# Attention two groups ahead, Newton runs for two groups, reordered routing steps, short POOL pauses, and expert products three blocks ahead

## The chip, the cores and the metric

The kernel runs on one core of one Trainium2 chip. The metric is the time on the device in microseconds (us). TensorE is called PE here, VectorE DVE, ScalarE ACT, GpSimd POOL and SyncE SP, as in the profile.

## The reference, cut to what matters

Activations are 64 x 64 tokens of width 128 (4096 tokens), all in float32.

```
K = ctx;  Q = layernorm(x)
scores = tril(K K^T)                        # per batch entry of 64 tokens, no softmax
x = x + tanh(g_xattn) * (Q + scores Q)
z = layernorm(x)
shared = silu(z sw1^T) sw2^T                # hidden width 512
top 2 of z gate_w^T over 8 experts; gates = softmax of the two logits
expert_e = silu(z w1_e^T) w2_e^T            # hidden width 512
x = x + tanh(g_ffn) * (shared + sum over the two experts of gate * expert_e)
```

Only the two chosen experts count for a token, so the kernel sends token rows to per-expert regions, multiplies whole blocks of 128 rows of one expert, and sends the rows back.

## The kernel before, in words

The 4096 tokens are 32 tiles of 128, in 8 groups of 4 tiles. There is a **first stage** (attention, layernorm, routing and the shared expert) and an **expert stage** of 71 blocks of 128 rows.

*First stage, PE* (`score`, `apply_scores`, `transpose_n`, `logits`, `positions`, `shared_units`). Each of 8 steps s runs apply_scores(s+1), transpose_n(s), score(s+2), logits(s), positions(s) and seven "units". A unit is one quarter of a group's shared expert: an even one is an up product (`ps_sup`), an odd one a down product (`ps_so`) of the group before. There are 72 units in all; `units_of(step)` deals them out, 7 a step from step 1. What is left runs after step 7, and units 64 to 71 (four down products) run between the first up products of the expert stage. `keep_warm` matmuls fill holes at the start.

*First stage, DVE* (one queue, in program order, step s): `residual(s+1)` (attention output added, statistics of the sum), `mask_scores(s+2)`, `choose(s)` (copy the logits out of PSUM, top 8, indices, one-hot, a running count), `statistics1(s+3)`, `norms` (a Newton run for 1/sqrt, 13 small instructions each waiting for the last, for the first layernorm of group s+3 and the second one of group s+1), and `place(s)`, which turns PE's `positions` into row numbers (`slot`) and releases POOL. The first groups' 1/sqrt runs on POOL (`norm`).

*First stage, ACT*: `centre_and_scale(g)` writes q, `normalise(g)` writes n, `evacuate_nT`, and `after_units` (silu of the up products, copies of the shared result into `shared`).

*POOL* scatters rows of n to DRAM, one indirect DMA for each tile and expert choice (`scatter_x`), with a `pause` (a memset of `spacer`, 128x400, on whose end the queue waits) after every second one. Groups 0 to 3 have 8 scatters each, groups 4 to 7 have 4 (together 48, part 0); 12 more of part 1 follow and four are spread over the expert stage. There `scatter_y(b)` sends the result rows of a block back.

*Between the stages.* After `place(7)` DVE runs `count_rows`, `place_second`, `tables_full` (rows and experts of the first 40 blocks; `tables_done` 1) and `tables_rest` (the others). SP waits for `tables_done`, loads the weights w1 of four blocks, waits until all 48 part-0 scatters have landed (`x_scattered[0]`), loads the rows of blocks 0 to 3 (`load_x(0)`), two more w1, then `load_x(1)` and `load_x(2)`. A set is four blocks; `transpose_rows(s)` transposes its rows and `evacuate_xT(s)` (DVE) copies them out of PSUM.

*Expert stage, PE*: transposes of set 0, up(0), up(1), units 64 to 71, transposes of set 1, a wait for all of `shared_out`, and then for each block b up(b+2) and down(b). `silu` and `evacuate_y` are ACT's. The last output groups are loaded, added and stored at the end.

Names and lines that matter: L426 pause, L420 scatter_x, L293 load_w1, L302 load_x, L615 residual, L607 mask_scores, L630 the logits copy, L572 statistics, L592 to L599 norms, L664 the first instruction of place, L674 and L676 the slots, L709 the end of a table, L776 evacuate_xT, L818 score, L828 apply_scores, L835 transpose_n, L844 logits, L869 and L877 units, L919 transpose_rows, L935 up, L944 down.

## Time and profile before

| | |
|---|---|
| three runs, us | 281.13, 277.95, 277.69; median 277.95 |
| the profiled execution, us | 278.51, of it 276.8 between first and last instruction (the span) |
| PE / PE weight loads busy | 244.2 us (88%) / 215.4 us (78%) |
| DVE / ACT / POOL busy | 129.4 (47%) / 132.0 (48%) / 178.4 us (64%) |
| mean granted PE clock | 0.949 |
| chain that ended last, by engine | PE 73%, DVE 10%, issue 5%, ACT 3%, POOL 3%, DMA 2%, unknown queue 2% |
| DMA | 46.94 MB, mean 170 GB/s |

The chain is the work followed back from the last instruction. The busy shares are means over two stages that differ, so they are to be read by stretch. A granted clock of 1.00 is 2.4 GHz, 0.50 is 1.2 GHz.

### The profile page before, as it was taken

How to read it: one execution, taken by the hardware profiler on the slowest of the kernel's cores; microseconds unless marked ns; L12 is line 12 of the kernel's file. 1: busy time of each engine (PE TensorE's matmuls, PEld its weight loads, DVE VectorE, ACT ScalarE, POOL GpSimd, SP SyncE). 2: the span in 40 equal slices, each digit the busy share in tenths (PEclk: the TensorE clock that was granted, in tenths of full speed). 3: DMA queues.
4: the chain of work that ended last, by engine and by line, in shares of the span. 5: the costliest groups of instructions: out<-in, count | busy, mean ns of one | idle time of the engine just before them, and what ended most of it. 6: DMA issues, size and time to landing. Idle time of an engine off the chain costs nothing.

```text
span 276.8 us, 6393 instructions
## 1 busy us (share of the span) xinstructions
PE 244.2 (88%) x1805; PEld 215.4 (78%) x1805; DVE 129.4 (47%) x576; ACT 132.0 (48%) x293; POOL 178.4 (64%) x249
## 2 busy tenths in 40 slices
PE   8789478999799799984999999999999999999910
PEld 4566266778578477784999999999999999999810
DVE  3959968678867668711321122223221101148203
ACT  1573262554545444422455456555555565555510
POOL 5674878668754367874678888887776545455430
PEclk9979979689889999998999999999999999999995
DMA  6992111111110011865766777776777767899827
GB/s 209 402 375 90 39 51 45 45 41 39 40 41 20 20 43 48 242 166 136 199 150 203 227 229 227 214 228 208 211 217 218 227 206 199 243 279 370 303 67 266
DMA packets 32625, 46.94 MB, mean 170 GB/s; under 512 B 5472, under 2 KB 16480, under 8 KB 32336
## 3 DMA queue, kind: packets, MB, share of 16 engines
q1 hardware_dynamic: 27264, 35.45, 42.7%
q0 software_dynamic: 4320, 8.99, 9.2%
q10 hardware_dynamic: 1008, 2.10, 2.0%
q8 instruction: 16, 0.26, 0.4%
q14 instruction: 17, 0.14, 0.2%
HBM read 34.43 MB, written 12.09 MB: 168 GB/s over the span
## 4 chain that ended last, share of the span: by engine, by line
PE 73%; DVE 10%; issue 5%; ACT 3%; POOL 3%; DMA 2%; another core or an unknown queue 2%; SPq 0%; POOLq 0%; DVEq 0%
PE bank L935 23%; PE bank L944 23%; PE bank L877 7%; PE bank L869 7%; PE bank L818 3%; PE bank L844 3%; PE bank L919 3%; ACT n L492 2%; PE bank L835 2%; DMA nT<-y_rows 2%; PE bank L884 1%; POOL rstd L378 1%; PE bank L828 1%; DVE top_at L636 1%
## 5 line engine op out<-in xcount | busy, mean ns | idle before, releaser
L452 POOL DMA_INDIRECT y_rows<-y,dest x71 | 69.9, 984 | 45.3 <-ACT y L548 30.6
L420 POOL DMA_INDIRECT expert_rows<-n,slot x64 | 63.1, 985 | 35.2 <-issue 15.9
L935 PE MATMUL bank<-xT,w_ring 128*128 128x128 f32 x568 | 76.2, 278 | 5.5 <-ACT kT L509 3.6
L944 PE MATMUL bank<-w,hT 128*128 x568 | 75.6, 277 | 0.0
L935 PEld LDWEIGHTS bank<-xT,w_ring 128*128 128x128 f32 x568 | 69.8, 194 | 6.5 <-issue 6.4
L944 PEld LDWEIGHTS bank<-w,hT 128*128 128x128 f32 x568 | 69.8, 194 | 0.0
L542 ACT ACTIVATE hT<-bank 128x512 f32<-128x512 f32 x71 | 42.4, 597 | 39.8 <-PE bank L935 27.0
L776 DVE COPY xT<-bank 128x512 f32<-128x512 f32 (+1 forms) x18 | 12.3, 684 | 98.4 <-PE bank L919 53.5
L877 PEld LDWEIGHTS bank<-sw,sT 128*128 128x128 f32 x256 | 33.5, 196 | 11.1 <-issue 11.1
L548 ACT ACTIVATE y<-bank,gate 128x128 f32<-128x128 f32 x71 | 26.1, 367 | 23.0 <-PE bank L944 13.6
L877 PE MATMUL bank<-sw,sT 128*128 128x128 f32 x256 | 34.5, 281 | 0.0
L869 PE MATMUL bank<-nT,sw 128*128 128x512 f32 x64 | 34.4, 625 | 0.0
L506 ACT ACTIVATE sT<-bank 128x512 f32<-128x512 f32 x32 | 19.0, 593 | 30.0 <-PE bank L869 26.1
L426 POOL MEMSET spacer<- 128x400 f32 x70 | 31.2, 446 | 0.1
L492 ACT ACTIVATE n<-xres,shift,rstd 128x128 f32<-128x128 f32 x32 | 13.2, 482 | 15.8 <-DVE shift L599 8.6
L835 PE MATMUL bank<-ident,n 128*128 128x128 f32 x32 | 9.2, 335 | 9.2 <-issue 5.3
L572 DVE BATCH_NORM_STATS2 stats<-xres 128x6 f32<-128x128 f32 x64 | 13.9, 280 | 3.0 <-DMA xres<-in_xP 2.6
L835 PEld LDWEIGHTS bank<-ident,n 128*128 128x128 f32 x32 | 4.4, 146 | 13.3 <-issue 8.7
L482 ACT ACTIVATE q<-xres,shift,rstd 128x128 f32<-128x128 f32 x32 | 13.1, 482 | 2.7 <-POOL shift L379 2.7
L818 PEld LDWEIGHTS bank<-kT 128*128 128x128 f32 x64 | 12.3, 269 | 0.7
L792 DVE TENSOR_TENSOR xres<-xres,nT 128x512 f32<-128x512 f32 x8 | 5.5, 692 | 14.4 <-DMA nT<-y_rows 12.7
L818 PE MATMUL bank<-kT 128*128 128x128 f32 x64 | 12.1, 354 | 0.0
(124 smaller groups left out, 229.7 us busy)
## 6 DMA issues: line engine op xcount, KB each, us to landing
w_ring<-in_w1T SPq DMA_DIRECT2D x71, 256.0 KB
x_ring<-expert_rows SPq DMA_DIRECT2D x71, 66.0 KB
w<-in_w2T SPq DMA_DIRECT2D x2, 1024.0 KB, 15.7
kT<-y_rows SPq DMA_DIRECT2D x8, 256.0 KB
nT<-y_rows SPq DMA_DIRECT2D x8, 256.0 KB, 3.8
out<-xres SPq DMA_DIRECT2D x8, 256.0 KB
xres<-in_xP SPq DMA_DIRECT2D x3, 512.0 KB, 10.2
kT<-in_ctxT ACTq DMA_DIRECT2D x3, 512.0 KB, 10.8
```

What stands on the lines that cost most here:

```text
L420: pool.indirect_dma_start(out=x_dram[:, :], out_offset=bass.IndirectOffsetOnAxis(ap=slot[:, i, k:k + 1], axis=0), in_=n[:, i, :], in_offse ...
L426: chained(pool.memset(spacer[:, :], 0.0))
L452: pool.indirect_dma_start(out=y_dram[:, :], out_offset=bass.IndirectOffsetOnAxis(ap=dest[:, b:b + 1], axis=0), in_=y[:, j], in_offset=None ...
L506: act.activation(sT[:, g % 2, j // 2], ps_sup[i % 2][:, :], ACT.Silu).then_inc(sT_done, 1)
L542: act.activation(hT[:, b % UP_SLOTS], ps_up[b % UP_SLOTS][:, :], ACT.Silu).then_inc(hT_done, 1)
L548: act.activation(y[:, b % Y_RING], ps_y[b % 2][:, 0:D], ACT.Copy, scale=gate[:, b:b + 1]).then_inc(y_done, 1)
L818: last = pe.matmul(ps_s[:, t * P:(t + 1) * P], k_t, k_t, start=False, stop=(t == G - 1), skip_group_check=True)
L835: last = pe.transpose(ps_n[:, t * P:(t + 1) * P], n[:, g * G + t, 0:D], ident[:, :])
L869: pe.matmul(ps_sup[i % 2][:, :], sw1[:, j // 2 * P:(j // 2 + 1) * P], nT[:, group(g)], start=True, stop=True).then_inc(sup_psum, 1)
L877: last = pe.matmul(ps_so[(g - 1) % 2][:, cols], sT[:, (g - 1) % 2, c, cols], sw2[:, c * D:(c + 1) * D], start=(c == 0), stop=(c == HC - 1))
L935: last = pe.matmul(ps_up[b % UP_SLOTS][:, cols], w1_ring[:, b % W_RING, cols], xT[:, s % X_SETS, i * P:(i + 1) * P], start=True, stop=True)
L944: last = pe.matmul(ps_y[b % 2][:, 0:D], hT[:, b % UP_SLOTS, c * P:(c + 1) * P], w2[:, ds(at + c * D, D)], start=(c == 0), stop=(c == HC - 1))
```

## The change

* Inputs: the loads of context groups 2 to 7 move from ACT's queue to SP's, and SP issues everything from group 2 on only when x of group 1 has landed.
* DVE: `choose` reads the logits from PSUM without the copy. Attention runs two groups ahead (`residual(s+2)`, `mask_scores(s+3)`). `norms` works on two groups at a time, in odd steps only. In even steps the order is choose, mask, residual, place, statistics of two groups; in odd steps residual, norms, choose, mask, place. `tables_rest` moves behind `evacuate_xT(0)`.
* PE: apply_scores(s+2) and score(s+3) in step s. Units begin in step 0: `UNTIL` puts 7, 14, 20, 27, 33, 40, 46, 52 of them behind the steps 0 to 7 (before: 0, 7, 14, 21, 28, 35, 42, 49). In odd steps all seven stand ahead of `positions`, in even ones three. 28 warm matmuls (8, 8, 3, 5, 4) in place of 29 (8, 5, 6, 10).
* POOL: a pause after every scatter, of 128x100. SP: two w1 loads ahead of `load_x(0)` instead of four and six behind it (the ring has 8 slots); the fills of region ends come one in two blocks from block 4.
* Expert stage: up products three blocks ahead, three PSUM banks for down products (`Y_SLOTS`), one bank instead of two for row transposes, transposes six blocks ahead; the wait for the last `shared_out` moves to block 1.

The diff, cut ("..." marks what is left out):

```diff
-    W_RING = 6
+    W_RING = 8
...
-    UP_AHEAD = 2
+    UP_AHEAD = 3
+    Y_SLOTS = 3
...
-    T_AHEAD = 5
+    T_AHEAD = 6
...
-    PER_STEP = 7
+    UNTIL = (7, 14, 20, 27, 33, 40, 46, 52)
...
-            return range((step - 1) * PER_STEP, min(UNITS * (GROUPS + 1), step * PER_STEP)) if step < GROUPS \
-                else range((GROUPS - 1) * PER_STEP, UNITS * (GROUPS + 1))
+            return range(UNTIL[step - 1] if step else 0, UNTIL[step])
...
+                if i == 2:
+                    sp.wait_ge(x_in[1], 16)
...
+                if i >= 2:
+                    sp.dma_start(kT[:, a * GW:b * GW], ctxT[:, a * GW:b * GW]).then_inc(ctx_in[i], 16)
...
-            for b in range(SET):
+            for b in range(2):
...
-            for b in range(SET, W_RING):
+            for b in range(2, W_RING):
...
-            sp.wait_ge(end_row_done, 1)
-            sp.wait_ge(tables_done, 2)
...
             for b in range(USED):
...
-                if b < E:
-                    fill_end(b)
+                if b == 4:
+                    sp.wait_ge(end_row_done, 1)
+                if b % 2 == 0 and 0 <= b // 2 - 2 < E:
+                    fill_end(b // 2 - 2)
...
+                        sp.wait_ge(tables_done, PARTS)
...
+            norm2(1)
...
-            norm2(1)
...
-                    if i % 2 == 1:
-                        pause()
+                    pause()
...
-                if i % 2 == 1:
-                    pause()
+                pause()
             def scatter_y(b):
...
+            act.dma_start(kT[:, GW:2 * GW], ctxT[:, GW:2 * GW]).then_inc(ctx_in[1], 16)
...
-            for i in range(1, len(LOADS)):
-                a, b = LOADS[i][0] * GW, LOADS[i][1] * GW
-                act.dma_start(kT[:, a:b], ctxT[:, a:b]).then_inc(ctx_in[i], 16)
...
+            centre_and_scale(2)
             for s in range(GROUPS):
...
-                if in_range(s + 2):
-                    centre_and_scale(s + 2)
-                some = units_of(s) if s > 0 else range(0)
-                after_units(some[:PER_STEP - 2])
-                if in_range(s + 1):
-                    normalise(s + 1)
-                after_units(some[PER_STEP - 2:])
-            after_units(range((GROUPS - 1) * PER_STEP, UNITS * GROUPS))
+                some = units_of(s)
+                if s % 2 == 0:
+                    if s == 0:
+                        normalise(1)
+                    if in_range(s + 3):
+                        centre_and_scale(s + 3)
+                    after_units(some[:4])
+                    if s > 0 and in_range(s + 1):
+                        normalise(s + 1)
+                else:
+                    after_units(some[:4])
+                    if in_range(s + 1):
+                        normalise(s + 1)
+                    if in_range(s + 3):
+                        centre_and_scale(s + 3)
+                after_units(some[4:])
+            after_units(range(UNTIL[-1], UNITS * GROUPS))
...
-                act.activation(y[:, b % Y_RING], ps_y[b % 2][:, 0:D], ACT.Copy, scale=gate[:, b:b + 1]).then_inc(y_done, 1)
-            for b in range(UP_AHEAD):
+                act.activation(y[:, b % Y_RING], ps_y[b % Y_SLOTS][:, 0:D], ACT.Copy, scale=gate[:, b:b + 1]).then_inc(y_done, 1)
+            for b in range(UP_AHEAD - 1):
...
+            silu(UP_AHEAD - 1)
             for b in range(USED):
...
-            def norms(slot, kinds):
-                out, var = rstd[:, slot, kinds], var_eps[:, slot, kinds]
-                bits, sq = half_bits[:, kinds], square[:, kinds]
-                chained(dve.tensor_scalar(var, mv[:, slot, kinds, :, 1], EPS, None, ALU.add))
+            def norms(slots, kinds):
+                out, var = rstd[:, slots, kinds], var_eps[:, slots, kinds]
+                bits, sq = half_bits[:, :, kinds], square[:, :, kinds]
+                chained(dve.tensor_scalar(var, mv[:, slots, kinds, :, 1], EPS, None, ALU.add))
...
-                return dve.scalar_tensor_tensor(out=shift[:, slot, kinds], in0=mv[:, slot, kinds, :, 0], scalar=-1.0,
+                return dve.scalar_tensor_tensor(out=shift[:, slots, kinds], in0=mv[:, slots, kinds, :, 0], scalar=-1.0,
...
-                dve.tensor_copy(logit[:, j], ps_logit.rearrange("p (t e) -> p t e", e=E)).then_inc(logit_read, 1)
-                dve.wait_ge(logit_read, g + 1)
...
-                    dve.max(out=top[:, g * G + t, :], in_=logit[:, j, t, :]).then_inc(top_done, 1)
+                    dve.max(out=top[:, g * G + t, :], in_=ps_logit[:, t * E:(t + 1) * E]).then_inc(top_done, 1)
...
-                    dve.max_index(out=top_at[:, j, t, :], in_max=top[:, g * G + t, :], in_values=logit[:, j, t, :])\
+                    dve.max_index(out=top_at[:, j, t, :], in_max=top[:, g * G + t, :], in_values=ps_logit[:, t * E:(t + 1) * E])\
...
-            mask_scores(0)
...
+            mask_scores(0)
+            mask_scores(1)
+            residual(0)
+            for_power(second(0)).then_inc(stats2_done, 1)
...
-            residual(0)
-            for_power(second(0)).then_inc(stats2_done, 1)
-            mask_scores(1)
+            residual(1)
+            for_power(second(1)).then_inc(stats2_done, 1)
+            mask_scores(2)
...
             for s in range(GROUPS):
-                if in_range(s + 1):
-                    residual(s + 1)
-                if s == 0:
-                    for_power(second(1)).then_inc(stats2_done, 1)
-                if in_range(s + 2):
-                    mask_scores(s + 2)
-                choose(s)
-                if s > 0 and in_range(s + 3):
-                    statistics1(s + 3)
-                    norms(s + 3, slice(0, 2)).then_inc(newton, 1)
-                elif s > 0 and in_range(s + 1):
-                    norms(s + 3, slice(0, 1)).then_inc(newton, 1)
-                place(s)
+                if s % 2 == 0:
+                    choose(s)
+                    if in_range(s + 3):
+                        mask_scores(s + 3)
+                    if in_range(s + 2):
+                        residual(s + 2)
+                    place(s)
+                    for g in (s + 4, s + 5):
+                        if in_range(g):
+                            statistics1(g)
+                else:
+                    if in_range(s + 2):
+                        residual(s + 2)
+                    if in_range(s + 1):
+                        norms(slice(s + 3, s + 5), slice(0, 2) if in_range(s + 3) else slice(0, 1)).then_inc(pairs_done, 1)
+                    choose(s)
+                    if in_range(s + 3):
+                        mask_scores(s + 3)
+                    place(s)
...
-            tables_rest()
             def evacuate_xT(s):
...
-                dve.tensor_copy(xT[:, s % X_SETS, 0:blocks * P], ps_x[s % 2][:, 0:blocks * P]).then_inc(xT_done, 1)
+                dve.tensor_copy(xT[:, s % X_SETS, 0:blocks * P], ps_x[:, 0:blocks * P]).then_inc(xT_done, 1)
...
+                    if b + T_AHEAD == 0:
+                        tables_rest()
...
+            keep_warm(8)
+            score(1)
+            apply_scores(0)
+            keep_warm(3)
+            apply_scores(1)
+            score(2)
...
-            apply_scores(0)
-            score(1)
-            keep_warm(6)
             for s in range(GROUPS):
-                if in_range(s + 1):
-                    apply_scores(s + 1)
+                some = units_of(s)
+                if s % 2 == 1 and in_range(s + 2):
+                    apply_scores(s + 2)
...
-                if in_range(s + 2):
-                    score(s + 2)
-                some = units_of(s) if s > 0 else range(0)
-                early = 0 if in_range(s + 2) else 1
-                shared_units(some[:early])
+                if s == 0:
+                    keep_warm(4)
+                elif in_range(s + 3):
+                    score(s + 3)
+                else:
+                    shared_units(some[:1])
...
-                    keep_warm(10)
-                shared_units(some[early:4])
+                    score(3)
+                rest = some if in_range(s + 3) else some[1:]
+                if s % 2 == 0 and in_range(s + 2):
+                    apply_scores(s + 2)
+                early = 7 if s % 2 == 1 and in_range(s + 2) else 3
+                shared_units(rest[:early])
...
-                shared_units(some[4:6])
...
+                    shared_units(rest[early:early + 2])
...
-                shared_units(some[6:])
-            shared_units(range((GROUPS - 1) * PER_STEP, UNITS * GROUPS))
+                    shared_units(rest[early + 2:])
+                else:
+                    shared_units(rest[early:])
+            shared_units(range(UNTIL[-1], UNITS * GROUPS))
             def transpose_rows(s):
-                at_least(pe, xT_done, s - 1)
+                at_least(pe, xT_done, s)
...
-                    last = pe.transpose(ps_x[s % 2][:, i * P:(i + 1) * P], x_ring[:, j, 0:D], ident[:, :])
+                    last = pe.transpose(ps_x[:, i * P:(i + 1) * P], x_ring[:, j, 0:D], ident[:, :])
...
-                at_least(pe, y_done, b - 1)
+                at_least(pe, y_done, b - Y_SLOTS + 1)
...
-                    last = pe.matmul(ps_y[b % 2][:, 0:D], hT[:, b % UP_SLOTS, c * P:(c + 1) * P], w2[:, ds(at + c * D, D)],
+                    last = pe.matmul(ps_y[b % Y_SLOTS][:, 0:D], hT[:, b % UP_SLOTS, c * P:(c + 1) * P], w2[:, ds(at + c * D, D)],
...
-            for b in range(UP_AHEAD):
+            for b in range(UP_AHEAD - 1):
...
-            pe.wait_ge(shared_out, GROUPS)
+            pe.wait_ge(shared_out, GROUPS - 1)
+            up(UP_AHEAD - 1)
             for b in range(USED):
...
+                if b == 1:
+                    pe.wait_ge(shared_out, GROUPS)
...
```

## Rows read from the trace of the kernel before

**Rows 1.** Windows (stretch, length, busy us of each engine, granted clock, DMA share, GB/s).
```profile
117.00:133.00 16.00, 11.66 (x88) 11.22 (x87) 2.52 (x10) 4.34 (x9) 9.86 (x13) 0.89 0.64 159
133.00:262.00 129.00, 127.84 (x1141) 127.30 (x1141) 35.25 (x100) 72.44 (x169) 87.97 (x112) 1.00 0.76 231
```

**Rows 2.** Timeline of PE (start, us, line, operation, count; idle before): step 4, full clock.
```profile
61.50 1.05 PE L828 MATMUL bank<-q,scores 128*128 128x128 f32 x8
62.39 0.60 PE L835 MATMUL bank<-ident,n 128*128 128x128 f32 x4
62.83 0.38 PE L814 MATMUL bank<-ident 128*128 128x512 bf16 x1
...
63.94 0.96 PE L844 MATMUL bank<-gT,nT 128*128 128x8 f32 x8
64.75 1.14 PE L877 MATMUL bank<-sw,sT 128*128 128x128 f32 x8
65.72 1.02 PE L869 MATMUL bank<-nT,sw 128*128 128x512 f32 x2
```

**Rows 3.** Timeline of DVE: step 2, from one residual to the next.
```profile
35.87 0.74 DVE L615 SCALAR_TENSOR_TENSOR xres<-bank,tanh_g,xres 128x512 f32<-128x512 f32 x1
...
39.77 0.69 DVE L607 TENSOR_TENSOR scores<-bank,mask 128x512 f32<-128x512 f32 x1 [1.84 <-PE bank L818]
40.76 0.19 DVE L630 COPY logit<-bank 128x32 f32<-128x32 f32 x1 [0.30 <-PE bank L844]
...
45.35 0.17 DVE L592 TENSOR_SCALAR var_eps<-mv 128x8 f32<-128x8 f32 x1
...
47.97 0.18 DVE L664 TENSOR_TENSOR where<-bank,region_row 128x32 f32<-128x32 f32 x1
...
48.63 0.74 DVE L615 SCALAR_TENSOR_TENSOR xres<-bank,tanh_g,xres 128x512 f32<-128x512 f32 x1
```

**Rows 4.** Timeline of PE, then the window around it (columns as in rows 1).
```profile
48.73 1.39 PE L835 MATMUL bank<-ident,n 128*128 128x128 f32 x4 [1.61 <-ACT n L492]
...
48.00:54.00 6.00, 5.16 (x22) 4.34 (x23) 3.77 (x19) 4.20 (x10) 3.88 (x6) 0.70 0.12 38
```

**Rows 5.** Timeline of POOL: a small memset, the first scatter, and two scatters with their pause.
```profile
3.12 0.20 POOL L369 MEMSET mask<- 128x128 f32 x1
...
24.34 1.19 POOL L420 DMA_INDIRECT expert_rows<-n,slot  x1 [2.77 <-DVE slot L674]
...
50.76 0.96 POOL L420 DMA_INDIRECT expert_rows<-n,slot  x1 [0.31 <-issue]
51.72 0.45 POOL L426 MEMSET spacer<- 128x400 f32 x1
...
53.71 0.96 POOL L420 DMA_INDIRECT expert_rows<-n,slot  x1 [0.30 <-issue]
```

**Rows 6.** Timelines of DVE, SP and PE between the two stages.
```profile
102.58 0.19 DVE L676 TENSOR_REDUCE slot<-placed 128x4 int32<-128x32 f32 x1
...
116.33 0.17 DVE L709 TENSOR_SCALAR weight_at<-expert_of 1x31 int32<-1x31 f32 x1
...
109.39 2.87 SPq L293 DMA_DIRECT2D w_ring<-in_w1T  x4
112.99 2.53 SPq L302 DMA_DIRECT2D x_ring<-expert_rows  x4
...
117.65 7.27 SPq L302 DMA_DIRECT2D x_ring<-expert_rows  x8
...
118.47 2.05 PE L935 MATMUL bank<-xT,w_ring 128*128 128x128 f32 x16 [0.78 <-issue]
...
128.09 1.34 PE L935 MATMUL bank<-xT,w_ring 128*128 128x128 f32 x8 [3.55 <-ACT kT L509]
```

**Rows 7.** The chain of waits near the end (start, us, what): a scatter's landing.
```profile
265.31 2.24 DMA y_rows<-y,dest
```

**Rows 8.** Timeline of POOL beside the table work: the longer of the two slow scatters.
```profile
112.40 1.65 POOL L420 DMA_INDIRECT expert_rows<-n,slot  x1 [0.28 <-issue]
```

18 lines of the change are left out of this document (8 added, 10 removed).

## The prediction

> **What bounds the kernel now.** I read the windows first. From 133 to 262 us PE is busy 127.84 of 129 us at a granted clock of 1.00: the expert stage is as dense as its matmuls allow, and nothing in the change takes a matmul out of it. In front of it, from 117 to 133 us, PE is busy 11.66 of 16 us [rows 1]. So time can come only from when the expert stage starts, and from the 14.8 us after it, which the change leaves alone.
>
> Then the timeline of PE in a step of the first stage. At full clock, start to start: apply_scores 0.89 (62.39 - 61.50), transpose_n 0.44, score 1.11, logits 0.81, together 3.25 us; a down unit 0.97 and an up unit about as much less a tenth, 0.9 us for a unit on the mean [rows 2]. With seven units a step needs 3.25 + 6.3 = 9.6 us of PE.
>
> The timeline of DVE for step 2 goes from 35.87 to 48.63, 12.76 us, of which it is idle 1.84 and 0.30: 10.6 us of work [rows 3]. So neither engine is full: DVE waits for PE's score and logits, and PE then waits for the normalised rows that hang on DVE's norms. A wait of PE of 1.61 us stands in front of a stretch with a granted clock of 0.70, so between two levels, 1.2 and 2.4 GHz, it lost 0.30 x 6 = 1.8 us more there [rows 4]. The steps from the first scatter (24.34) to the last slots (102.77) take (102.77 - 24.34)/7 = 11.2 us each [rows 5, 6]. That is what the change works on: the loss is a chain that runs from PE to DVE to ACT and back once a step.
>
> **The change part by part.**
>
> *DVE in a step.* The norms take 47.97 - 45.35 = 2.62 us; one run for two groups halves that, -1.31 us a step (16 elements instead of 8 in instructions of 0.17 us, which I take as free; bound: +0.05 us in each of 13). The logits copy goes, 40.76 to its end 0.19 and a gap, -0.2 us; max and index then read PSUM, bounded by nothing and by the 0.2 us saved. 10.6 - 1.5 = 9.1 us a step while attention runs, less in steps 4 to 7, where statistics and then residuals run out [rows 3].
>
> *PE in a step.* 3.25 + 0.9 x 6.5 = 9.1 us in the mean. So both engines need about 9.1 us, and running attention two groups ahead gives each something to do while the other is late. I walked the queues with these durations. Start: the input order and warm matmuls differ, but the chain statistics, POOL's 1/sqrt, q, attention, residual, n of group 0 keeps its length; the first slots come at 25.4, or 27 if the clock is half there; I take 26 against 24.0. Steps 1 to 3: DVE is full (9.1) and PE's score(s+3) waits once a pair of steps for mask_scores, 1.1 us, and positions waits 0.5 to 2 us for choose in odd steps: 10.3 us a step, last slots of group 3 at 57. Steps 4 to 7: PE bounds, 8.65 (six units), 2.14 + 6.3 = 8.4 (no score), and twice 1.25 + 5.4 = 6.65, less 1.8 us that PE is ahead by: 28.5 us. Slots of group 7 at 85.6, against 102.8.
>
> *POOL now bounds.* Two scatters and a pause take 53.71 - 50.76 = 2.95 us. A memset of 128x400 takes 0.45, one of 128x128 0.20, and one of 128x100 will be near 0.18 (bounds 0.10 and 0.20). A scatter with its pause: 0.96 + 0.18 + 0.28 (the gap behind a pause, 2.95 - 0.96 - 0.45 - 0.96 - 0.30) = 1.42 us, hardly less than the 1.48 of now. 48 of them from 26.3 on: 26.3 + 68.2 = 94.5, while the slots come early enough after group 1 to keep the queue fed [rows 5]. The last one lands 2.24 us later as a scatter does at the end of the kernel [rows 7]: 96.8. The other path to the first row loads: slots 85.6, tables 109.39 - 102.77 = 6.6, two w1 loads of 2.87/4 = 0.72: 93.7. So load_x(0) is issued at 96.8 (112.99 before) [rows 6]. Both paths are equal when slots of group 7 come at 88.3; later than that, every us counts.
>
> Two scatters of the trace are longer, 1.65 us at most, and both lie beside the table work of DVE [rows 8]; beside DVE's small instructions they take 0.96, and so the sum has 0.96 for all 48. The Trainium skill, SBUF — State Buffer, section "Who interferes with whom", says that a GpSimd instruction and a copy, cast or tensor_scalar of DVE in a two-port form shut each other out for the whole instruction. By it a fuller DVE would stretch POOL's chain, which now sets the end of the stage; by the rows nothing is added. What it would come to is rival C.
>
> *Between the stages.* PE's units after logits(7): 5 + 12 = 17, so 15 us, against 21 before; logits(7) ends near 81 and PE is through at 96: it idles until the rows land. Issue of four x loads 2.53 -> 99.3. Before, the last of them was issued by 115.5, and up(0) started at 118.47 after transposes (0.44) and the 0.78 of the copy, so a landing costs at most 118.47 - 1.22 - 115.5 = 1.7 us -> 101.0; transposes and copy 1.2 -> 102.2 [rows 6]. up(0) and up(1) take 2.05 less a tail, 1.8 us, at full clock and 3.6 at half; PE has idled 5 us before, so I take 3.0 -> 105.2. Units 64 to 71, four down products of 0.9: 108.8. Meanwhile SP issues six w1 (6 x 0.72 = 4.3) and set 1 (4 x 7.27/8 = 3.6) -> 107.2, landed 108.9, transposed 109.3. up(2) starts at 109.5, against 128.09 before: -18.6 us. tables_rest now lies behind the copy of set 0; it takes the time from the first table, which lets SP go at 109.39 or some tenths before, to 116.5, 7 to 8 us [rows 6], so from 102.2 to 110.2, and the copy of set 1 is done at 111.0; up(4), the first to need it, comes after up(2), up(3) and down(0) at 112.2: hidden with 1.2 us to spare, and if PE is earlier than that it costs the difference.
>
> *The clock behind it.* Before, the expert stage began at half clock after 3.55 us of idle; the stretch 117 to 133 shows 0.89, 1.8 us lost [rows 1, 6]. With up(2) right behind the units this is not paid: -1.8.
>
> *The unexplained wait.* PE's 3.55 us were charged to a copy by ACT that itself had nothing visible to wait for. By the arithmetic above set 1 was in by 117.65 + 3.6 + 1.7 = 123.0. I can't name it. Its bounds after the change are 0 and about 2.7 us; as the wait for the last shared_out moves behind two up products, I take 0.7.
>
> *Expert stage.* Three ahead, three banks, eight w1 slots: PE has 1.2 us of idle in 129 us, so at most that is gained; a block needs its x and w1 as many blocks ahead as before or more. One bank for the transposes asks DVE for a copy of 0.7 us every four blocks (7.6 us): nothing. The part-1 scatters follow at 94.5 and take 12 x 1.42 = 17 us, until 111.5; the first y is due at 112. Nothing.
>
> **The sum.** 276.8 - 18.6 - 1.8 + 0.7 = 257.1 span. The profiled execution takes 1.7 us more than its span (278.51) and stands 0.6 us above the median. 258.8 us. About 2%, 5.6 us, is what a measurement of this kernel can tell from no change.
>
> **The rivals.**
>
> *A, the clock.* The waits of PE in odd steps (up to 2 us) are of the size of the one that stood before the stretch at 0.70 [rows 4]. If six steps lose 1.8 us each, slots of group 7 come at 96.4, 8.1 behind the 88.3 from which it counts: 258.8 + 8.1 = 267. For it: it happens now. Against it: a wait of 1.1 us has no such row, and POOL covers the first 2.7 us. 19%.
>
> *B, the steps stay as long.* PE and DVE wait for each other in a ring, so that only the place of the waits moves. At 11.2 us a step slots of group 7 come at 26 + 78.4 = 104.4, load_x(0) at 112.5, up(2) at 125.2: 276.8 - 2.9 - 1.8 + 1.7 + 0.7 = 274.5. If DVE's 9.1 and PE's front part 3.25 lie wholly in line, 12.35 a step, it is 282.6. Both within 2% (the first by 0.6%). 10%, since the norms and the copy do leave DVE's queue.
>
> *C, slower: POOL's scatters stretch.* DVE would be nearly full, and two of 64 scatters, beside table instructions of 0.9 us, took up to 1.65 instead of 0.96 us [rows 8]. At +0.69 for each of 48 POOL ends at 94.5 + 33.1 = 127.6, and up(2) starts 33.1 later, at 142.6: 258.8 + 33.1 = 291.9. It is slower by 2% from +0.53 us each (25.3 us), that is if three scatters in four are hit. Against it: the other 62 scatters took 0.96 beside the same small instructions. 4%.
>
> *D, as forecast.* 67%, with a range of its own from 253 to 263: low with a pause of 0.10 us (-3.8, of which 3.1 until the tables bind), full clock at up(0) (-1.2) and some of the idle in the expert stage (-1); high with first slots at 27, the whole unexplained wait (+2) and a landing 1 to 2 us longer.
>
> **How the numbers follow.** The time is D's. The range 253 to 269 takes in D but for a twentieth and nearly all of A: about 8 in 10. Faster by over 2% are D and A, 0.86; within 2% is B, 0.10; slower is C, 0.04.
>
> **What the profile after would show.** POOL: scatters at a distance of 1.42 us without a gap from group 2 on, the 48th near 94 us; if slots of group 7 come after 88 and the scatters have gaps, A or B holds. DVE: one run of norms per two groups, instructions still 0.17 us; the span from residual to residual near 10 us in steps 1 to 3. load_x(0) at 97, up(2) at 109.5, the stretch behind it at a clock of 1.00, and 147.6 us from up(2) to the end (148.7 before). The prediction is wrong if load_x(0) waits for something else than the scatters' landing, if PE waits at set 1 for its w1 or rows, or if the expert stage shows idle that it did not have.

## The result, and the profile after

The changed kernel takes 281.12 us (median of 20 runs, 277.78 to 284.94) against 277.79 for the kernel before (20 runs, 274.82 to 281.13): ratio 1.012, 95% interval 1.009 to 1.015. It is slower by 1.2%, less than the 2% that the prediction took as what one measurement can tell, but twenty runs of each set it apart from no change; 258.8 us, faster by 7%, was forecast. Ratios, here and below, leave out executions more than 1.5% above the fastest of the same kernel. The profiled execution took 280.87 us, its span is 279.1.

The page of the changed kernel, part 1 (busy time, share and instructions of each engine):

```profile
PE 242.8 (87%) x1804; PEld 213.6 (77%) x1804; DVE 118.4 (42%) x529; ACT 129.3 (46%) x293; POOL 164.8 (59%) x279
```

DVE's work shrank from 129.4 to 118.4 us, as costed. The span did not. The hole opens in step 3 of the first stage. PE, DVE and ACT in the timelines of the changed kernel (start, duration, idle time before and what ended it):

```profile
46.11 1.06 PE L846 MATMUL bank<-q,scores 128*128 128x128 f32 x8
47.01 0.60 PE L853 MATMUL bank<-ident,n 128*128 128x128 f32 x4
...
47.66 1.05 PE L836 MATMUL bank<-kT 128*128 128x128 f32 x8
52.88 1.88 PE L862 MATMUL bank<-gT,nT 128*128 128x8 f32 x8 [4.16 <-issue]
```
```profile
51.60 0.75 DVE L625 SCALAR_TENSOR_TENSOR xres<-bank,tanh_g,xres 128x512 f32<-128x512 f32 x1 [2.84 <-remote]
```
```profile
52.23 0.60 ACT L496 ACTIVATE nT<-bank 128x512 f32<-128x512 f32 x1 [3.80 <-remote]
```

apply_scores (L846) ends in PE's record at 46.11 + 1.06 = 47.17, and transpose_n (L853) at 47.61. DVE's residual and ACT's evacuate_nT wait for just these two, are free from 48.76 and 48.43 on, and start at 51.60 and 52.23: 4.4 and 4.6 us late. PE's logits (L862) need ACT's copy, so PE idles 4.16 us, and the stretch behind it runs at half clock, each matmul taking twice its time (1.88 for L862 against the 0.96 of logits at full clock [rows 2]). In the trace's list of semaphore updates PE's own come late here (4.3 and 4.6 us behind the records' ends), while those of ACT, DVE and POOL come on time. I call this a **hold-up**. The profile can't find a releaser for such a wait and writes "remote" or "issue". The Trainium skill, Perfetto Trace Analysis, section "Per-engine timelines", says that TensorE's end time is estimated by the profiler and not observed; the trace agrees, since here 4.4 us lie between a record's end and what it releases. So it is not shown whether PE itself stood still or only its updates did. The window behind it (us, then busy time and count of PE, PE's weight loads, DVE, ACT and POOL, granted clock, DMA share, GB/s) has a clock of 0.66, 3.4 us lost:

```profile
50.00:60.00 10.00, 7.12 (x23) 5.24 (x24) 7.56 (x42) 1.19 (x2) 8.05 (x15) 0.66 0.14 47
```

There is another near 77 to 82 us, and smaller ones at 96 to 103, 116 to 124 and 140 to 175. POOL, in its timeline (scatter, pause, scatter; a first scatter that waited for slots):

```profile
39.13 0.96 POOL L423 DMA_INDIRECT expert_rows<-n,slot  x1 [0.71 <-issue]
40.09 0.20 POOL L429 MEMSET spacer<- 128x100 f32 x1
40.56 0.96 POOL L423 DMA_INDIRECT expert_rows<-n,slot  x1 [0.28 <-issue]
...
88.69 0.96 POOL L423 DMA_INDIRECT expert_rows<-n,slot  x1 [6.37 <-DVE slot L684]
```

A scatter and its pause take 1.43 us, as forecast, but POOL waits for late slots (6.37 us here) and so does not bound. Between the stages, SP and PE:

```profile
109.25 2.91 SPq L304 DMA_DIRECT2D x_ring<-expert_rows  x4
112.89 4.02 SPq L295 DMA_DIRECT2D w_ring<-in_w1T  x6
```
```profile
116.63 3.78 PE L964 MATMUL bank<-xT,w_ring 128*128 128x128 f32 x16 [2.03 <-DVE xT L792]
120.21 4.06 PE L895 MATMUL bank<-sw,sT 128*128 128x128 f32 x31
...
125.86 1.95 PE L964 MATMUL bank<-xT,w_ring 128*128 128x128 f32 x16
```

load_x(0) comes at 109.25 (before 112.99), up(2) at 125.86 (before 128.09) [rows 6]. The expert stage then gives it back. A window of the changed kernel there, same columns, to hold against 127.84 of 129 us before [rows 1]:

```profile
160.00:180.00 20.00, 17.12 (x147) 16.35 (x146) 3.89 (x12) 9.17 (x25) 12.54 (x21) 1.00 0.66 184
```

The list of waits shows where releasers have no name (engine, line, releaser: us in total, times, longest). These us are the whole idle time of the engine in front of the instruction, much of which it would have spent anyway; how late an update is stands only in the list of updates. The changed kernel, then the kernel before:

```profile
DVE xT L792 <- remote: 20.4, 3, 7.2
...
ACT hT L551 <- remote: 10.3, 3, 4.6
...
ACT kT L508 <- remote: 6.2, 3, 3.0
...
ACT nT L496 <- remote: 5.4, 2, 3.8
```
```profile
DVE xT L776 <- remote: 8.5, 1, 8.5
ACT kT L509 <- remote: 7.9, 2, 5.7
```

The second row of the kernel before is the copy of the shared result for which PE waited 3.55 us at up(2), the wait that the prediction could not name [rows 6]: PE's updates in front of it are up to 3.1 us late, so it was a hold-up already.

### The profile page after: what moved, and what is told of

Same layout as the page of the kernel before. It is cut to its first block, busy times and chain, and to the rows that moved or that the text cites. A ratio compares the mean times of both kernels' runs of the same rounds, so it can differ in the third digit from the quotient of the medians.

```text
span 279.1 us, 6374 instructions
## 1 busy us (share of the span) xinstructions
PE 242.8 (87%) x1804; PEld 213.6 (77%) x1804; DVE 118.4 (42%) x529; ACT 129.3 (46%) x293; POOL 164.8 (59%) x279
## 4 chain that ended last, share of the span: by engine, by line
PE 69%; DVE 11%; issue 6%; DMA 5%; ACT 3%; SPq 2%; POOL 1%; DVEq 0%; another core or an unknown queue 0%; POOLq 0%; ACTq 0%
PE bank L964 24%; PE bank L973 21%; PE bank L895 7%; PE bank L887 6%; PE bank L948 3%; PE bank L862 3%; DVE stats L582 2%; PE bank L846 2%; DMA nT<-y_rows 2%; DMA xres<-in_xP 1%; ACT n L491 1%; POOL y_rows L453 1%; ACT q L481 1%; PE bank L836 1%; DVE mv L585 1%
## 5 line engine op out<-in xcount | busy, mean ns | idle before, releaser
L964 PE MATMUL bank<-xT,w_ring 128*128 128x128 f32 x568 | 77.7, 281 | 7.3 <-issue 3.8
L423 POOL DMA_INDIRECT expert_rows<-n,slot x64 | 61.9, 967 | 32.7 <-issue 13.0
L792 DVE COPY xT<-bank 128x512 f32<-128x512 f32 (+1 forms) x18 | 12.3, 683 | 101.1 <-PE bank L948 46.6
L895 PEld LDWEIGHTS bank<-sw,sT 128*128 128x128 f32 x256 | 35.1, 203 | 12.9 <-issue 12.4
L895 PE MATMUL bank<-sw,sT 128*128 128x128 f32 x256 | 35.9, 287 | 1.1 <-issue 1.1
L429 POOL MEMSET spacer<- 128x100 f32 x100 | 19.7, 197 | 0.1
L862 PEld LDWEIGHTS bank<-gT,nT 128*128 128x128 f32 x64 | 8.9, 215 | 10.6 <-issue 7.4
L862 PE MATMUL bank<-gT,nT 128*128 128x8 f32 x64 | 9.4, 273 | 8.1 <-issue 5.6
L582 DVE BATCH_NORM_STATS2 stats<-xres 128x6 f32<-128x128 f32 x64 | 13.9, 280 | 2.9 <-DMA xres<-in_xP 2.6
L948 PE MATMUL bank<-ident,x_ring 128*128 128x128 f32 x71 | 11.8, 279 | 1.6 <-DMA x_ring<-expert_rows 1.2
L948 PEld LDWEIGHTS bank<-ident,x_ring 128*128 128x128 f32 x71 | 8.5, 142 | 3.8 <-DMA x_ring<-expert_rows 2.0
L887 PEld LDWEIGHTS bank<-nT,sw 128*128 128x128 f32 x64 | 10.6, 205 | 1.0 <-ACT sT L505 0.5
```

The source lines that it names most:

```text
L423: pool.indirect_dma_start(out=x_dram[:, :], out_offset=bass.IndirectOffsetOnAxis(ap=slot[:, i, k:k + 1], axis=0), in_=n[:, i, :], in_offse ...
L429: chained(pool.memset(spacer[:, :], 0.0))
L582: dve.bn_stats(stats[:, which, g % 2, t, :], xres[:, tile(g, t)]).then_inc(part_done, 1)
L862: last = pe.matmul(ps_logit[:, t * E:(t + 1) * E], nT[:, tile(g, t)], gT[:, :], start=True, stop=True)
L887: pe.matmul(ps_sup[i % 2][:, :], sw1[:, j // 2 * P:(j // 2 + 1) * P], nT[:, group(g)], start=True, stop=True).then_inc(sup_psum, 1)
L895: last = pe.matmul(ps_so[(g - 1) % 2][:, cols], sT[:, (g - 1) % 2, c, cols], sw2[:, c * D:(c + 1) * D], start=(c == 0), stop=(c == HC - 1))
```

## Experiments

They ran on five chips, and what ran on one shares the runs of the kernel before: runs 1 to 4 on chip I (before 276.4 us), 5 to 8 on II (277.6), 9 to 12 on III (281.5), 13 to 16 on IV (275.8), 17 and 18 on V (278.8).

**Chance or the kernel, and which half?** Runs 1 and 2 repeat the changed kernel and the one before.

> The changed kernel, unchanged, on another chip or at another time. Two theories on why the first stage kept its length. H (hold-ups): semaphore updates of PE reach ACT and DVE up to 5 us after the matmul's record (47.2 to 51.5 us, 120.5 to 123.9 us in the profile after) and half clock follows; where they fall changes from run to run. D (dependencies): the new order itself makes PE wait at fixed places. By H the long idle of PE (4.2 us before the logits of group 3) is somewhere else or gone in this trace, and transposes of n in step 4 start anywhere from 55 to 64 us; by D they start at 63 to 64 us again, behind the same wait. Ratio 1.00 to 1.02 by both.

280.51 us, ratio 1.015 (1.008 to 1.023). Hold-ups at the same places, 49 to 63, 78 to 85 and 99 to 103 us; the idle before the logits of group 3 is 2.29 us instead of 4.16.

> The kernel before, unchanged, for a second trace. H: late updates of PE occur here too, at other places than 121 to 127 us; the 5.7 us wait of ACT at 121.2 us is not in it. D: that wait is there again at the same place. Time 275 to 280 us.

276.97 us. Few hold-ups in the first stage, and the one ahead of up(2) at the same place (125 us, up to 2.5 us late). So the late updates are those of H, but their places stay, as D had it: with one trace more of each kernel, where they fall looks like a matter of the kernel and not of chance.

Run 3 takes the first stage and the pauses of the change, run 4 only its expert stage:

```diff
 run 3: -    UP_AHEAD = 3   run 4: +    UP_AHEAD = 3
        +    UP_AHEAD = 2          +    W_RING = 8
        -    W_RING = 8            +    Y_SLOTS = 3
        +    W_RING = 6            ... (rest as before)
```

> The change's first stage and POOL pauses with the expert stage of before (two up products ahead, two banks each, six weight slots, tables in one piece, four w1 loads ahead of the rows). If the expert stage of the change is what costs: 0.96 to 0.98 (272 us or less). If the first stage gives nothing and the expert stage nothing: 1.00. If the first stage costs and the expert stage is neutral: 1.01, as the whole change.

284.21 us, ratio 1.027 (1.020 to 1.034).

> The first stage and pauses of before with the change's expert stage and its SP order. If the expert stage of the change costs: 1.01 to 1.03, with up(2) to the end over 150 us (148.7 before, 153.2 after). If it is neutral: 1.00, 148 to 149 us from up(2) to the end.

275.08 us, 0.991 (0.983 to 1.000). So the expert stage's edits cost nothing and bring a little at most, and the loss is all in the first stage's edits or the pauses. Run 3 is slower than any theory had it. In it even the old expert stage takes 138.0 us from up(2) to the last up product, 132.9 before; what it has of the change there is the pause of 128x100, for one of 128x400, behind each scatter of y.

**The pauses.** Run 5 is the change with the old pauses, run 6 the kernel before with the new ones:

```diff
 run 5 (changed kernel)                  run 6 (kernel before)
-  spacer = sb("spacer", [P, 100])       -  spacer = sb("spacer", [P, 400])
+  spacer = sb("spacer", [P, 400])       +  spacer = sb("spacer", [P, 100])
-                    pause()             -                    if i % 2 == 1:
+                    if i % 2 == 1:      -                        pause()
+                        pause()         +                    pause()
```

> The changed kernel with the pauses of the kernel before: one memset of 128x400 after every second scatter in place of one of 128x100 after every one. Theory P (the short pauses, one behind every scatter, make PE's updates late and lengthen the expert stage): the hold-ups of PE near 47 to 63 us and 77 to 84 us go, slots of group 7 come at 86 to 92 us instead of 101 to 104, the stretch from up(2) to the last up product returns from 135.6 to 133 us, and the time is 265 to 271 us. Rival O (the order of PE's and DVE's work makes them, pauses have nothing to do with it): slots of group 7 at 100 to 104 us, hold-ups at the same places, time 279 to 283 us.

272.49 us, 0.987 (0.980 to 0.995), slots of group 7 at 97.5: faster than before, and by the ratios 2.5% faster than with the short pauses. Theory P had more (265 to 271 us, slots at 86 to 92): hold-ups of up to 3.4 us stay near 54.

> The kernel before with the short pauses of the change (128x100 after every scatter). Theory P: it is slower than before by 4 to 8 us (281 to 285), with hold-ups in the first stage and an expert stage of 135 us or more from up(2) to the last up product. Rival O: no difference that can be measured, 276 to 278 us, expert stage 133 to 134 us.

282.63 to 288.84 us in four runs, median 287.56, against 277.62: slower by 1.8% at least, with not one edit of order in it. Its timelines show the same picture with the old order (PE idle 3.55 us at logits; DVE's residual waited 3.98 us and starts 3.2 us behind the end of apply_scores in PE's record):

```profile
51.82 1.17 PE L842 MATMUL bank<-gT,nT 128*128 128x8 f32 x8 [3.55 <-issue]
```
```profile
49.75 0.75 DVE L613 SCALAR_TENSOR_TENSOR xres<-bank,tanh_g,xres 128x512 f32<-128x512 f32 x1 [3.98 <-remote]
```

The pauses make the loss. Their scatters stand 1.44 us apart, evenly, where the old pauses have 1.27 and 1.68 in turn, 1.47 on the mean.

**How far apart?** Runs 9 to 12, one chip: no pause, 128x400 behind every scatter, 128x400 only behind the scatters of y, 128x200 behind every scatter.

```diff
 run 9:  -   pause()      (all three places)
 run 10: -   spacer = sb("spacer", [P, 100])      +   spacer = sb("spacer", [P, 400])
 run 11: -                if b < FULL: pause()    +                if b < FULL: pause(400)
 run 12: -   spacer = sb("spacer", [P, 100])      +   spacer = sb("spacer", [P, 200])
```

> The changed kernel without any pause: scatters at a distance of 0.96 + 0.30 = 1.26 us where rows are ready. Theory Q (a scatter right on the heels of another makes PE's updates late; the longer POOL stays away from the next scatter, the less): hold-ups of PE longer than in the changed kernel, slots of group 7 at 105 us or later, more than 136 us from up(2) to the last up product, time 286 to 296 us. Rival E (the even distance of short pauses is what hurts, or the memsets themselves): as fast as with the long pauses, 270 to 276 us.

> The changed kernel with a pause of 128x400 behind every scatter: a distance of 0.96 + 0.45 + 0.28 = 1.69 us, even. Theory Q: late updates of under 2 us, slots of group 7 at 90 to 95 us; POOL's 48 scatters take 81 us from 26.9 on and land at 110 us, so that load_x(0) comes at 108 to 111 as now and up(2) at 120 to 124; 131 to 133 us of expert stage; time 266 to 272 us. Rival E: even distances hurt at any length, 278 us or more.

> The changed kernel with short pauses (128x100) in the first stage and pauses of 128x400 behind the scatters of y. Theory Q: the first stage as in the changed kernel (slots of group 7 at 101 to 104 us), the expert stage with 132 to 133 us from up(2) to the last up product instead of 135.6: 277 to 278 us. Rival: the expert stage is longer because of how the first stage ends, then it stays at 135.6 and the time at 281.

> The changed kernel with 128x200 behind every scatter: memset near 0.28, distance near 1.52 us. Theory Q with a gradual effect: between the changed kernel and long pauses behind all, 272 to 277 us, slots of group 7 at 94 to 99. If there is a limit between a distance of 1.44 and 1.47 us (the long pauses behind every second scatter have 1.47 on the mean): as good as 272.5 or better, slots at 97 or earlier. Rival E: 278 or more.

| pause behind a scatter | distance, us | ratio to before | slots of group 7, us | up(2) to last up, us |
|---|---|---|---|---|
| none (9) | 1.26 | 1.041 (1.031 to 1.051) | 108.9 | 134.3 |
| 128x100 (the change; 1; 17) | 1.44 | 1.012; 1.015; 1.029 | 101.1; 103.7; 107.0 | 135.9; 135.6; 135.1 |
| 128x400 after every second (5) | 1.27, 1.68 | 0.987 (0.980 to 0.995) | 97.5 | 132.4 |
| 128x200 (12) | 1.52 | 0.973 (0.964 to 0.982) | 96.8 | 134.3 |
| 128x400 (10) | 1.69 | 0.983 (0.975 to 0.990) | 90.9 | 132.8 |

Windows of PE in the first stage, 50 to 90 us: without pauses, then with 128x400 behind every scatter:

```profile
50.00:90.00 40.00, 30.97 (x164) 24.09 (x164) 20.94 (x116) 16.03 (x35) 19.35 (x21) 0.83 0.11 36
```
```profile
50.00:90.00 40.00, 38.84 (x262) 30.91 (x263) 30.07 (x173) 22.91 (x48) 33.33 (x49) 1.00 0.13 42
```

The changed kernel has 33.91 busy us at a clock of 0.87 there. The times are 293.04 us (run 9), 276.11 (run 10) and 273.19 (run 12), against 281.53 before. Run 10 has no update over 0.2 us late before 137 us, and the place that opened the hole reads so in its PE and DVE timelines:

```profile
49.84 1.06 PE L846 MATMUL bank<-q,scores 128*128 128x128 f32 x8
50.73 0.60 PE L853 MATMUL bank<-ident,n 128*128 128x128 f32 x4
...
52.27 0.96 PE L862 MATMUL bank<-gT,nT 128*128 128x8 f32 x8
```
```profile
51.40 0.75 DVE L625 SCALAR_TENSOR_TENSOR xres<-bank,tanh_g,xres 128x512 f32<-128x512 f32 x1
```

The residual starts 0.5 us behind the record's end instead of 4.4, and PE doesn't idle. The first stage is 10 us shorter, but 48 scatters at 1.69 us now reach to 108, and load_x(0) is issued at 109.71: the gain is handed to POOL. Hence 128x200 is the best of the row, if by little (all four runs of 12, 271.76 to 275.13 us, lie under the four of 10, 275.38 to 276.72): hold-ups of up to 3.4 us are left between 59 and 73 us, but POOL is earlier (load_x(0) at 105.57). Theory Q holds from run to run in the first stage; the rival E (even distances hurt) falls with runs 10 and 12. Two of Q's forecasts were missed: run 9's expert stage took 134.3 us and not over 136, and run 10 took 276.11 us and not 266 to 272. Run 11 measured 285.39 us, 1.018 (1.009 to 1.026), where Q wanted 277: its expert stage did shrink to 131.4 us, but its first stage had larger hold-ups than the changed kernel's (slots at 107.7), with the same code there. Whether that is the chip or the small shift isn't known: the changed kernel itself did not run on chip III. On that chip the row of slots is 108.9 without pauses, 107.7 with 128x100, 96.8 with 128x200 and 90.9 with 128x400.

**The other half: PE's work.** Run 7 puts all units behind the steps, run 8 one step later.

```diff
-    UNTIL = (7, 14, 20, 27, 33, 40, 46, 52)
+    UNTIL = (0, 0, 0, 0, 0, 0, 0, 0)      (run 7)
+    UNTIL = (0, 7, 14, 21, 28, 35, 42, 49) (run 8)
```

> The changed kernel with no unit of the shared expert in steps 0 to 7 (all 72 stand behind logits(7)); the same work in all. PE has then 3.25 us of matmuls in a step and waits the rest. Theory L (PE is held up when it has run densely for some us, whatever DVE and POOL do): no update of PE comes over 1 us late in the first stage, although the clock is half in much of it; steps of DVE's length, 9 to 10.5 us. Rival R (the ring PE to DVE to ACT to PE takes 12 us, the units don't matter): steps of 11 to 12.5 us as now, slots of group 7 at 101 or later. Rival S (POOL's scatters hold PE's updates up): late updates of 3 to 5 us stay at the same places. The time is worse than now in all cases, about 60 x 0.9 = 54 us more less what the steps give back, as the units then lie behind.

312.83 us. Windows of the first stage:

```profile
50.00:90.00 40.00, 21.06 (x97) 18.44 (x96) 29.06 (x172) 11.82 (x28) 32.22 (x57) 0.50 0.14 47
```

With the scatters as close as in the change, PE at half clock and half idle has one late update of 0.2 us up to 100 us, and slots of group 7 come at 90.4, eleven us earlier than in the change, though its matmuls take twice as long. Scatters alone don't do it (rival S falls), nor is the ring long by itself (rival R falls). The units that stand behind the steps show the rest in the same trace. From 90 us on PE is dense again, and POOL's scatters go on, 1.44 us apart, until 114. PE idles there for 1.80 and 3.03 us, behind updates up to 4.1 us late. Once the scatters are over, PE runs 30 us without a gap:

```profile
110.00:120.00 10.00, 6.97 (x23) 4.32 (x22) 0.00 (x0) 2.37 (x4) 3.49 (x6) 0.69 0.32 84
120.00:150.00 30.00, 30.00 (x171) 21.89 (x170) 0.00 (x0) 12.91 (x21) 0.00 (x0) 0.99 0.00 1
```

So within one run: scatters beside a PE with gaps, no hold-up; a dense PE with scatters, hold-ups; a dense PE without scatters, none. The loads stop with the scatters (1 GB/s from 120 us on, 84 before), so the last step parts PE from all DMA and not from scatters alone.

> The changed kernel with its units shared out as in the kernel before: none in step 0, seven in each step from 1 on, three more left over for behind step 7. Theory L: the first hold-up, at 47 us, moves to later or goes, since PE is less dense up to there; slots of group 7 at 92 to 98 us, time 272 to 278. Rival O in its form that two groups ahead make the ring longer whatever the units do: slots at 101 to 104 us and 281 us or more.

282.24 us, 1.021 (1.014 to 1.028), slots at 102.6: it didn't help, and the time is that of rival O. Less dense up to 47 us is not enough; theory L's forecast for this run was wrong. It shows nothing for rival O's ring, though, as the same hold-ups are in its trace (up to 3.4 us late near 57).

**Scatters away, other work, another pause.** Runs 13 to 16:

```diff
 run 13: -    pool.wait_ge(slots_done, g + 1)   +    pool.wait_ge(slots_done, GROUPS)
 run 14: the kernel before, with spacer [P, 200] and a pause() behind every scatter
 run 15: UNTIL all 0, and                       +    keep_warm(26)   ahead of positions(s)
 run 16: -    chained(pool.memset(spacer[:, :], 0.0))
         +    for _ in range(2): chained(pool.memset(spacer[:, 0:1], 0.0))
```

> The changed kernel, but POOL begins its scatters only once the slots of the last group are there; all else as it is. The whole takes some 50 us longer, since 48 scatters of 1.44 us then lie behind the steps. Theory Q (PE's updates come late where a dense PE meets scatters in close order): no update over 1 us late in the steps, steps as long as their work, slots of group 7 at 84 to 90 us, as the prediction's walk through the queues had them (85.6). Rival: the hold-ups come from PE's own density and merely lie on other places with other scatters; then up to 5 us late again near 47 to 60 and 77 to 84 us, slots at 98 to 104.

> The kernel before with 128x200 behind every scatter (its order, its units, its expert stage), distance 1.52 us. If the gain of the changed kernel with these pauses (0.973 of before) came from the pauses alone: 0.975 to 0.985 here. If it is the new order that gains once the hold-ups are small: 0.99 to 1.01.

> The changed kernel with the units of the shared expert behind the steps and, in each step in their place, 26 matmuls of 128x512 on constants that no one waits for (5.6 us at full clock): PE is dense again and its clock full, scatters 1.44 us apart. Theory Q in the form that PE's activity as such is the other half: late updates of 2 to 5 us in the first stage again. In the form that it is the weight loads and updates of the units: none over 1 us. The time is 50 to 70 us longer in both.

> The changed kernel with a pause made of two memsets of 128x1, one waiting for the other: hardly anything written, distance by estimate 1.5 to 1.65 us. If the distance of the scatters counts: 0.965 to 0.985 of before, slots of group 7 at 91 to 98 us. If what counts is that POOL is inside a long memset: as without pauses, 1.02 to 1.04.

Measured: 325.13 us; 270.72, ratio 0.981 (0.975 to 0.986); 302.81 us; 268.23, ratio 0.975 (0.971 to 0.980). Runs 13 and 15 are one execution each. Run 15 is 27 us longer than the kernel before, not 50 to 70, and run 16 has slots of group 7 at 86.8, earlier than forecast. None of the four has a single late update or a "remote" wait in its trace, run 15 with a dense PE and scatters 1.44 us apart among them. That was either the kernels or the chip, so runs 17 (the change) and 18 (run 15 again) went together on another.

> The changed kernel unchanged, on the same chip as the next run. If late updates of PE belong to its distance of 1.44 us: up to 4 or 5 us late between 45 and 85 us, slots of group 7 at 100 to 104, 1.00 to 1.02 of before. If they belong to some chips alone (the four runs of the call before this one had none): on a chip without them 0.96 to 0.98.

> Matmuls on constants in place of the units within the steps, units behind, once more, beside the changed kernel on the same chip. Activity theory: late updates of 2 to 5 us in the first stage, if the changed kernel has them here, slots of group 7 at 98 or later. Units theory: none over 1 us with slots at 92 to 96, although the changed kernel has them.

286.86 us, 1.029 (1.022 to 1.037), with slots at 107.0, and 326.8 us (one execution) for the very program that took 302.8 on chip IV. PE's timeline in run 15, then in run 18, at the same place:

```profile
50.60 1.05 PE L836 MATMUL bank<-kT 128*128 128x128 f32 x8
51.49 0.96 PE L862 MATMUL bank<-gT,nT 128*128 128x8 f32 x8
```
```profile
50.58 1.05 PE L836 MATMUL bank<-kT 128*128 128x128 f32 x8
58.59 1.88 PE L862 MATMUL bank<-gT,nT 128*128 128x8 f32 x8 [6.96 <-issue]
```

From 28 to 50.6 us PE's records in the two agree within 0.02 us (but for single matmuls without a record), then one idles 6.96 us. So hold-ups are in the traces of some chips (I, II, III, V and that of the changed kernel's profile) and not in the four of chip IV. The units are not the other half: in run 18 matmuls on constants, which no one waits for, stand in their place, and PE idles longer at one go than in any hold-up of another run's first stage. These matmuls load weights too (2012 weight loads in the trace of run 15, 1804 in that of the changed kernel), so PE's matmuls and weight loads are not parted.

**A rival that no run tests: the recording.** The traces of chip IV differ from all others in one more thing. They hold 6576 to 6702 semaphore updates each; the other sixteen hold 3490 to 4033. The same program left 6576 on chip IV (run 15) and 3513 on chip V (run 18). Where hold-ups are seen, then, four or nearly five in ten updates are missing from the trace, and the run with the fewest hold-ups, run 10, kept the most (4033; run 9 without pauses 3507). It may be that some chips hold PE up and lose records too, or that the recording of a dense PE beside many scatters is itself what holds PE up. Every timed execution has its span and granted clock on record, so none shows what the kernels take when nothing is recorded.

Runs 13 and 16 thus say nothing on theory Q: without hold-ups there was nothing to take away. Runs 14 and 16 show the orders side by side without the disturbance: 0.981 (0.975 to 0.986) of before for the old order, 0.975 (0.971 to 0.980) for the new, with nearly the same pauses. The intervals overlap, so the changed order and expert stage are worth 1% at most, and perhaps nothing. Run 14 also leaves a riddle. It differs from the kernel before in nothing but its pauses, and gained 1.9% on chip IV, as forecast if the pauses do it alone. If the kernel before had no hold-ups there, this gain has no explanation. No trace of it was taken on chip IV; its granted clock there (0.944 to 0.966; 0.967 to 0.974 in the four shorter executions of run 14, 0.943 and 0.950 in the two longer ones) hints that it lost time to half clock as elsewhere. So chip IV is free of hold-ups only as far as its four traces go, and the changed kernel itself never ran on it.

The best version measured is the changed kernel with 128x200: 0.973 (0.964 to 0.982) of before on a chip with hold-ups, an interval that overlaps those of runs 5 and 10; run 16, with distances of 1.5 us (1.86 where a group begins), has 0.975 on chip IV.

## Why the prediction was wrong, point by point

| | predicted | changed kernel | run 13 | run 16 |
|---|---|---|---|---|
| slots of group 3, us | 57 | 64.3 | 59.3 | 57.3 |
| slots of group 7, us | 85.6 | 101.1 | 90.0 | 86.8 |
| load_x(0), us | 96.8 | 109.25 | | 103.55 |
| up(2), us | 109.5 | 125.9 | | 118.2 |
| up(2) to the end, us | 147.6 | 153.2 | | 146.7 |
| span, us | 257.1 | 279.1 | | 264.9 |

The slots are the starts of their instructions; they end 0.2 us later.

* **The failed step is the price of the pause.** The prediction sized it as POOL's time alone ("0.96 + 0.18 + 0.28 = 1.42 us, hardly less than the 1.48 of now") and wrote nothing down for the spacing of scatters itself. The POOL time was right, 1.43 us; but with scatters at that distance PE's updates come late, the first stage ended at 101.1 in place of 85.6, and run 6 shows that the short pauses alone cost the kernel before 5 us at least (282.63 against 277.62) and up to 11. It was the smallest line of the diff.
* **Not the whole miss.** Run 16, without a hold-up, still has 7.8 us of span more than forecast. load_x(0) is 6.8 us late: its 48th scatter starts at 100.6 where 26.3 + 47 x 1.42 = 93.0 was meant (0.6 from the first scatter, 4.2 from the distance of 1.51 us in place of 1.42, 2.8 from longer distances, most of them 0.35 us more where a group begins), and 0.8 came back on the way to the landing. Another 1.9 us lie between load_x(0) and up(2), and 0.9 came back in the expert stage. Run 7, at the changed kernel's own distance and with no hold-up by then, issues load_x(0) at 98.5, 1.7 us behind the forecast: POOL's own time was costed well. The forecast time is also one of the profiled execution: the 0.6 us by which that stood above the median was named and not taken off.
* **The walk through the steps** (10.3 us each in steps 1 to 3, 28.5 for steps 4 to 7) stands where hold-ups are absent. Run 16 has group 7's slots 1.2 us behind it. Run 13, with no scatter near, is 4.4 us behind, 3.4 of it lost at half clock from 38 to 45 us, right behind waits of PE of 2.59 and 0.71 us in step 1. In the changed kernel step 3 took 16.7 us from transpose to transpose (8.8 in run 16) and step 4 13.9 (10.8); then 9.3 and 6.9 (7.7 and 6.9).
* **DVE's and PE's 9.1 us a step**: the terms held. Of the 13 norm instructions on 16 elements twelve take 0.17 to 0.19 us and one 0.31, and DVE lost 11.0 us of work. It was not what bounded.
* **POOL as the bound** was never reached in the changed kernel, as its waits for slots show. In run 10 it was, at 1.69 us.
* **Between the stages** the parts came out somewhat longer: load_x(0) to up(2) predicted 12.7, run 16 has 118.2 - 103.55 = 14.6, the changed kernel 16.6: 7.4 to up(0) for 5.4, 3.6 for up(0) and up(1) for 3.0, 5.2 for units 64 to 71 for 3.6, of it 1.06 of idle ahead of the last of them, and 0.4 for 0.7.
* **The clock behind up(2)** was not paid, as forecast: from 125.86 to 133 us PE is busy throughout at a granted clock of 1.00, where the kernel before had half clock from 128.9 to 132.3. It was paid ahead of it instead, half clock from 114.1 to 120.9 over up(0) and up(1), which took 3.6 us for 3.0.
* **The unexplained wait** was given 0.7 us. It was a hold-up, which before the change had cost PE 3.55 us at this place [rows 6]. Its bounds, 0 and 2.7 us, were taken from that one place instead of asking where else it could strike.
* **Expert stage, nothing**: 5.6 us longer. Without hold-ups (run 16) it is 0.9 shorter than the 147.6 forecast, so the deeper lookahead brings little, and in the changed kernel the late updates at 140 to 175 us take more than that.
* **Rivals.** A (half clock in odd steps) described what follows a hold-up, and priced too low what comes before it; it acts without one too, as run 13 shows. A counts from slots at 88.3, where both paths to load_x(0) are equal; by the prediction's own 96.8 and 93.7 that is 85.6 + 3.1 = 88.7, which moves A's time by 0.4 us. B's times (274.5, up to 282.6) lay nearest, by luck, as its mechanism did not act: from first scatter to last slots run 16 takes 60.1 us, 8.6 a step, where B had 11.2 and the forecast 8.5. C looked at POOL and the right instruction but the wrong victim: the scatters stayed at 0.96 us beside DVE (mean 967 ns over 64 in the changed kernel). The interference that the Trainium skill, SBUF — State Buffer, section "Who interferes with whom" describes between GpSimd and DVE shows in no scatter of the first stage here but, perhaps, the first one at 1.19, which was so before too [rows 5].

**What stays open.** How close scatters and a busy PE make PE's updates late is not shown, nor whether it is the chip or the recording of the trace that does it, nor why the traces of one chip have none. The distance is what was varied; the length of the memset varied with it in all runs on chips with hold-ups (and the old pauses, with every second distance at 1.27 us, did better than an even 1.44), and the run meant to part the two (16) fell on chip IV. Whether the order of the change brings more hold-ups than the old one at equal pauses is not settled either.

## What to carry to other kernels

A wait that the profile charges to "remote", or to a releaser that had long been done, is to be named before the kernel is changed around it: its price at one place says nothing of how often it can strike once the neighbours run closer. A pause that looks like waste in one engine's queue may protect another engine, so a change of it is tried alone, at several lengths. A ratio from one chip may miss an effect that others have: here one program took 302.8 us on one and 326.8 on another. And before two traces are compared, count what each holds: these two differed by nearly half of their semaphore updates.

## What the runs showed of the hardware that was not expected

* PE's semaphore updates came up to 5 us behind the end of the matmul's record in the changed kernel, in bursts, while ACT's, DVE's and POOL's came on time; in run 18 PE idled 6.96 us at one go for it. It is seen only in traces that lack many of their semaphore updates (they hold 3490 to 4033, those without hold-ups some 6600).
* It took both a busy PE (38 of 40 us where nothing disturbs it; no hold-up at 21 of 40) and POOL's indirect scatters close behind each other: at even distances the slots of group 7 came at 108.9 us for 1.26, 96.8 for 1.52 and 90.9 for 1.69, the last without a hold-up in the first stage. In run 7 a PE busy for 30.00 of 30 us with no scatter beside it had none.
* Behind the long ones the granted clock fell to 1.2 GHz, after PE had idled (4.16 us ahead of 52.9 in the changed kernel, half clock from 52.7 to 59.5).
* The traces of one chip of five showed none of it in four kernels, and these are the only ones with all updates.
